# A delta-rule core on one core: its loop of 67 turns written out, and masked copies over tiles that hold the identity in place of two products with it

## Chip, cores and metric

One Trainium2 chip, one of its cores. The metric is the device time of one execution of the whole kernel in microseconds, which is the span of that core; lower is better. Everything is one launch: eight sublayers of a small network over an activation X of 16 x 512 tokens x 128 channels, which stays on the chip between them.

## What is computed

The change touches one part of one sublayer, the chunked delta rule of `L1_attn_b`. There are 16 sequences, 4 heads of 32 channels and chunks of 32 tokens, so 16 chunks for each sequence:

```python
A = jnp.where(strict_lower, jnp.einsum('bhncd,bhnsd->bhncs', k_beta, k), 0.0)
attn_inv = jax.scipy.linalg.solve_triangular(eye + A, jnp.broadcast_to(eye, A.shape), lower=True)
u = attn_inv @ v
w = attn_inv @ k_beta
...
def step(S, inp):
    q_i, k_i, u_i, w_i = inp
    attn_local = jnp.where(incl_lower, q_i @ jnp.swapaxes(k_i, -1, -2), 0.0)
    u_t = u_i - w_i @ S
    o_i = q_i @ S + attn_local @ u_t
    return (S + jnp.swapaxes(k_i, -1, -2) @ u_t, o_i)
```

A is 32 x 32 for each chunk and head, strictly lower triangular; the state S is carried from chunk to chunk.

## The kernel before

The program is a row of stages, each with its own tiles and semaphores and a barrier at its end: attention with a mask (L0), the mixture of experts twice, window attention, attention with rotation, channel mixing twice, and the gated delta sublayer. The last consists of `delta_inputs` (q, k, v), `delta_core`, `long_filters` and `gated_sum`, one after the other. Nothing of another stage runs beside `delta_core`.

**Items and slots.** An item is one chunk of 4 sequences with 4 heads each: 16 blocks of 32 x 32, which fill a slot of 128 partitions (head and row) x 4 sequences x 32 columns. There are 64 items (4 groups of sequences x 16 chunks). `products` (L2424) is one product of slots: 16 matmuls of 32 x 32 in fp32. Each stands in the trace as two weight loads and two matmuls, so a product has 32 and 32 records.

**The inverse.** (I + A)^-1 is built from 2 x 2 blocks upward in levels: `first` is the gram matrix masked to the pairs, `U2` adds the identity. Then, for blocks of 4, 8, 16 and 32 (n = 0 to 3): a product of G1 or G2 (copies of the gram matrix) with U gives the block below the diagonal, DVE masks it out of PSUM into `N[n]` (`masked`, L2532; the masks hold -1 inside and 0 outside), a product of `N[n]` with the transposed T adds to T in PSUM, DVE turns the result by 32 x 32 transposes into `U[n]` (`turn`, L2535), and ACT copies it to `T_[n]`. The levels of 4 and 8 use the banks called early, those of 16 and 32 the ones called late, for the item before. Two products with the identity put the old T into PSUM ahead of the sum: `products(T_early, U2, eye, True)`, whose result ACT also copies to `T2`, and `products(T_late, U[1], eye, True)`; the level's own product then has `fresh` False.

**A turn.** The four engines run a loop of 67 turns (64 items and a lag of 3), in which each product serves another item: the early levels of one, the late levels of the one before, then w and u, then state and output of a third. The order within a turn is written by hand for every engine, and semaphores tie them together. PE has 18 products, DVE 13 operations, ACT 8 copies, POOL 7 operations (chunks of k, q, v out of a ring of tiles, G2, U2). SP is written out already: it fills the ring (3 transfers of 256 KB for 4 items) and stores each item's output in 4 transfers from `out`.

**The loop.** On PE, ACT and POOL it is `Fori(0, TURNS)`, on DVE a `Fori` of 3 turns and then, for each group, a `Fori` of 15 turns and one turn on its own that clears S. Waits are on values that come from the loop's register (`r + 1`, `r + 2`); to keep them positive, semaphores are raised by 1 ahead of the loop, and each group of waits ends with a `sem_inc(waited, 1)`.

Of the kernel before, what the change touches and what calls it, by code (L numbers as in the profile page):

```python
# [6 lines left out]
ACT = mybir.ActivationFunctionType  # L7
# [2284 lines left out]
def delta_core(nc, tag, io, kqv_dram, delta_dram):  # L2292
# [8 lines left out]
    TURNS, LAG = ITEMS + 3, 3  # L2301
    TILE_ITEMS = P // CHUNK
    with Stage(nc, tag) as s:
# [10 lines left out]
        local, w, S, u, out = slot("local"), slot("w"), slot("S"), slot("u"), slot("out")  # L2314
# [7 lines left out]
        kA_ready, qC_ready, kqvB_ready = s.sem("kA_ready"), s.sem("qC_ready_1"), s.sem("kqvB_ready_1")  # L2322
        K_ready, V_ready, G2_ready = s.sem("K_ready_1"), s.sem("V_ready_1"), s.sem("G2_ready_1")
        gram_done, first_ready, G_kept = s.sem("gram_done_1"), s.sem("first_ready_1"), s.sem("G_kept_1")
        U2_ready, T2_done, T2_kept = s.sem("U2_ready_1"), s.sem("T2_done_1"), s.sem("T2_kept_1")
        per_level = lambda name: [s.sem(f"{name}{n}_1_") for n in range(LEVELS)]
        N_done, N_kept = per_level("N_done"), per_level("N_kept")
        T_done, U_kept, T_kept = per_level("T_done"), per_level("U_kept"), per_level("T_kept")
        local_done, local_kept, q_used = s.sem("local_done_1"), s.sem("local_kept_1"), s.sem("q_used_1")
        w_done, w_kept, u_done, u_kept = s.sem("w_done_1"), s.sem("w_kept_1"), s.sem("u_done_1"), s.sem("u_kept_1")  # L2330
        S_done, S_kept, out_done, out_kept = (s.sem("S_done_1"), s.sem("S_kept_1"), s.sem("out_done_1"),
                                              s.sem("out_kept_1"))
        stored = s.sem("stored_4")
        waited = s.sem("waited")
# [9 lines left out]
        def chunk(x, m):  # L2344

            return ring[:, x, :, bass.ds(((m + CHUNKS) % CHUNKS) * CHUNK, CHUNK)]

        @block.sync
        def _(sp):
            sp.dma_start(masks[:, :, :], io["chunk_masks"].rearrange("m p i -> p m i")).then_inc(masks_in, 16)  # L2350
            sp.sem_inc(stored, 64 * (LAG + 1))
# [16 lines left out]
            for m in range(ITEMS):  # L2368
                group, k = m // CHUNKS, m % CHUNKS
                sp.wait_ge(out_kept, m + LAG + 2)  # L2370
                for h in range(DH):
                    rows = slice(CHUNK * h, CHUNK * h + CHUNK)
                    sp.dma_start(delta_dram[group * GROUP:(group + 1) * GROUP, k * CHUNK:(k + 1) * CHUNK, rows]
                                 .rearrange("b i d -> i b d"), out[rows, :, :]).then_inc(stored, 16)
                if m % TILE_ITEMS == 2 and m // TILE_ITEMS + TPS < GROUPS * TPS:
                    load(m // TILE_ITEMS + TPS)
                    if m // TILE_ITEMS + TPS == GROUPS * TPS - 1:
                        sp.sem_inc(ring_in, 48)
            sp.wait_ge(stored, 64 * (LAG + 1 + ITEMS))

        @block.gpsimd
        def _(pool):
# [6 lines left out]
            for sem in (qC_ready, kqvB_ready, G2_ready, U2_ready):  # L2389
                pool.sem_inc(sem, 1)  # L2390
# [5 lines left out]
            with pool.Fori(0, TURNS) as r:  # L2396
                pool.wait_ge(q_used, r + 2)
                pool.sem_inc(waited, 1)
                g.tensor_copy(qC[:, :, :], chunk(Q_ROW, r - 2)).then_inc(qC_ready, 1)
                pool.wait_ge(N_done[3], r + 2)  # L2400
                pool.sem_inc(waited, 1)
                g.tensor_copy(G2[:, :, :], G1[:, :, :]).then_inc(G2_ready, 1)
                pool.wait_ge(first_ready, r + 2)
                pool.sem_inc(waited, 1)
                g.tensor_tensor(U2[:, :, :], first[:, :, :], over(EYE), ALU.add).then_inc(U2_ready, 1)
                pool.wait_ge(gram_done, r + 2)
                pool.sem_inc(waited, 1)
                pool.wait_ge(ring_in, ((r + 1) // TILE_ITEMS) * 48 + 48)
                pool.sem_inc(waited, 1)
                g.tensor_copy(kA[:, :, :], chunk(K_ROW, r + 1)).then_inc(kA_ready, 1)  # L2410
                pool.wait_ge(V_ready, r + 2)
                pool.sem_inc(waited, 1)
# [5 lines left out]
        def _(pe):  # L2418
# [9 lines left out]
            eye = masks[:, EYE, :].unsqueeze(1).to_broadcast([P, GROUP, CHUNK])  # L2428
            for sem in (q_used, S_done, out_done, u_done, local_done, gram_done, T2_done, w_done, *N_done, *T_done):
                pe.sem_inc(sem, 1)  # L2430
# [4 lines left out]
            with pe.Fori(0, TURNS) as r:  # L2435
                now, before = r + 2, r + 1
                pe.wait_ge(U_kept[1], before)
                pe.wait_ge(G2_ready, before)
                pe.wait_ge(local_kept, before)
# [9 lines left out]
                pe.wait_ge(w_kept, before)  # L2449
                pe.wait_ge(S_kept, before)  # L2450
# [4 lines left out]
                pe.sem_inc(waited, 1)  # L2455
                products(T_late, N[2], T_[1], False).then_inc(T_done[2], 1)
                pe.wait_ge(qC_ready, before)
                pe.wait_ge(out_kept, before)
                pe.sem_inc(waited, 1)
# [3 lines left out]
                pe.sem_inc(waited, 1)  # L2463
                products(T_early, N[0], T2, False).then_inc(T_done[0], 1)
# [629 lines left out]
```

## Time and profile before

| | before |
|---|---|
| median of 3 runs | 5331.94 us (5324.82 to 5354.07) |
| the profiled execution | 5354.72 us, span 5352.7 us |
| busy over the span | PE 4147.9 us (77%), PE weight loads 2483.3, DVE 3059.4, ACT 2393.8, POOL 1809.8 |
| delta core | about 4259 to 4702 us of the span |
| PE records | 73,116 matmuls and 73,118 weight loads |
| mean granted clock of PE | 0.854 |

PE is TensorE's matmuls, PEld its weight loads, DVE VectorE, ACT ScalarE, POOL GpSimd, SP the engine that issues most DMAs. In the timelines a row merges neighbouring instructions of one kind: start, duration, and in brackets how long the engine was idle before it, and what ended that; "issue" means that nothing which the profile shows was awaited. The queues q8 and q14 bring instructions, q1 and q0 data.

### The profile page before, as it was taken

Reading aid. Unit: us, or ns where it says so; the run is one execution under the profiler, and the core shown is the slowest. Engines: PE = TensorE matmul, PEld = TensorE weight load, DVE = VectorE, ACT = ScalarE, POOL = GpSimd, SP = SyncE. Lnnn points to the kernel's source line nnn. Section 1 sums busy time; section 2 is a strip of 40 time slices with the busy share of each in tenths; the row PEclk is TensorE's granted clock in tenths of the full one; section 3 lists DMA queues with packets and bytes.
Section 4 is the critical chain, followed back from the end, with each engine's and each line's share of the span. In section 5 each row is a group of like instructions: output and inputs, shape, how many; then the busy total and the mean of one; then the engine's idle time right before and its main releaser. Section 6 shows DMA issues by size and latency. Waiting matters only on the chain. (4 is left out here: it accounts for less than half of the span.)

```text
span 5352.7 us, 179249 instructions
## 1 busy us (share of the span) xinstructions
PE 4147.9 (77%) x73116; PEld 2483.3 (46%) x73118; DVE 3059.4 (57%) x6496; ACT 2393.8 (45%) x5497; POOL 1809.8 (34%) x2620
## 2 busy tenths in 40 slices
PE   4898888448189999997291699999957799996555
PEld 1333333347045555555291233333345699984223
DVE  5555554434366666664344677777576555514887
ACT  1555555125145445552151377777735433313443
POOL 3343433130655555551405332222012233302442
PEclk9888887579599999997595799999877799997777
DMA  2111110211100000001111111111001211162001
GB/s 75 45 46 46 45 47 21 73 52 52 37 2 2 3 2 2 2 2 33 41 53 48 48 45 46 44 48 43 19 2 63 84 39 45 22 193 77 24 24 34
DMA packets 252942, 218.33 MB, mean 41 GB/s; under 512 B 63683, under 2 KB 221316, under 8 KB 252550
## 3 DMA queue, kind: packets, MB, share of 16 engines
q1 hardware_dynamic: 244358, 196.20, 12.1%
q0 software_dynamic: 8192, 16.79, 1.1%
q8 instruction: 259, 4.24, 0.3%
q14 instruction: 133, 1.09, 0.1%
HBM read 139.24 MB, written 73.14 MB: 40 GB/s over the span
## 5 line engine op out<-in xcount | busy, mean ns | idle before, releaser
L687 DVE TENSOR_REDUCE l_M<-l_max_bank 128x2 f32<-128x1024 f32 (+3 forms) x1024 | 1033.6, 1024 | 616.7 <-PE l_max_bank L501 381.7
L647 ACT ACTIVATE l_probs<-l_exp_bank 128x512 f32<-128x512 f32 (+3 forms) x2048 | 953.9, 520 | 632.8 <-PE l_exp_bank L517 622.6
L517 PE MATMUL l_exp_bank<-l_QS,l_KS 49*128 49x512 bf16 (+3 forms) x2048 | 667.4, 369 | 82.0 <-ACT l_probs L647 68.1
L495 PE MATMUL l_max_bank<-l_KS,l_QS 48*128 48x512 bf16 (+3 forms) x2048 | 611.5, 374 | 69.8 <-DMA l_KS<-l_parts_dram 45.2
L479 PE MATMUL l_out_bank<-l_probs,l_V 128*32 128x256 f32 (+2 forms) x6144 | 562.8, 448 | 23.0 <-ACT l_heads_out L603 20.8
L397 POOL TENSOR_SCALAR_AFFINE_SELECT l_probs<-l_probs 128x256 f32<-128x256 f32 x512 | 208.7, 408 | 543.1 <-ACT l_probs L647 540.6
L517 PEld LDWEIGHTS l_exp_bank<-l_QS,l_KS 49*128 49x128 bf16 x2048 | 177.0, 95 | 375.4 <-ACT l_probs L647 350.9
L495 PEld LDWEIGHTS l_max_bank<-l_KS,l_QS 48*128 48x128 bf16 x2048 | 156.4, 97 | 333.3 <-issue 165.7
L1841 DVE TENSOR_REDUCE l_M<-l_max_bank 128x4 f32<-128x512 f32 x256 | 175.5, 686 | 171.7 <-PE l_max_bank L1655 171.7
L871 POOL DMA_INDIRECT l_back<-main_sorted_out,l_index x128 | 122.6, 958 | 412.8 <-issue 412.8
L436 POOL TENSOR_TENSOR l_qk<-l_qk,l_cos 128x512 f32<-128x512 f32 x32 | 40.5, 1266 | 568.7 <-ACT l_rot L621 568.7
L479 PEld LDWEIGHTS l_out_bank<-l_probs,l_V 128*32 128x32 f32 x6144 | 135.0, 111 | 207.8 <-issue 164.2
L1496 POOL TENSOR_TENSOR l_rms<-l_rms,l_minus_half 128x20 f32<-128x20 f32 x64 | 226.2, 3535 | 11.8 <-POOL l_rms L1493 11.6
L501 PE MATMUL l_max_bank<-l_ident,l_mask 64*128 64x64 bf16 x2048 | 228.4, 208 | 0.0
L969 ACT ACTIVATE l_hidden<-l_up_bank,l_own 128x128 f32<-128x128 f32 x584 | 166.9, 368 | 86.7 <-PE l_up_bank L919 86.7
L1721 ACT ACTIVATE l_raw<-l_misc 128x512 f32<-128x512 f32 (+1 forms) x192 | 101.4, 528 | 222.1 <-PE l_misc L1558 220.8
L915 PE MATMUL l_t_bank<-main_identity,l_rows 128*128 128x128 f32 x148 | 49.4, 334 | 185.9 <-DMA l_rows<-main_sorted_in 185.9
L857 POOL DMA_INDIRECT main_sorted_in<-l_hn,l_index x128 | 124.7, 974 | 189.6 <-DVE l_hn L1000 151.2
L1633 PE MATMUL l_out_bank<-l_V,l_probs 64*64 64x65 f32 x2048 | 175.6, 226 | 1.3 <-issue 1.3
L1635 PE MATMUL l_out_bank<-l_V,l_probs 64*64 64x65 f32 x2048 | 175.6, 226 | 0.0
L1641 PE MATMUL l_out_bank<-l_V,l_probs 64*64 64x65 f32 x2048 | 175.6, 226 | 0.0
L501 PEld LDWEIGHTS l_max_bank<-l_ident,l_mask 64*128 64x128 bf16 x2048 | 160.7, 105 | 21.9 <-issue 7.0
(419 smaller groups left out, 10301.3 us busy)
## 6 DMA issues: line engine op xcount, KB each, us to landing
l_parts_dram<-l_parts SPq DMA_DIRECT2D x64, 384.0 KB, 2.6
l_fir_band<-in_dr_short_dram SPq DMA_DIRECT2D x16, 1024.0 KB, 6.6
l_fir_band<-in_dr_long_dram SPq DMA_DIRECT2D x16, 1024.0 KB, 8.9
l_QS<-l_parts_dram SPq DMA_DIRECT2D x128, 96.0 KB
l_KS<-l_parts_dram SPq DMA_DIRECT2D x128, 96.0 KB
l_kqv_dram<-l_in_out SPq DMA_DIRECT2D x16, 768.0 KB, 3.6
l_core_ring<-l_kqv_dram SPq DMA_DIRECT2D x48, 256.0 KB, 3.2
l_rows<-main_sorted_in SPq DMA_DIRECT2D x152, 64.0 KB, 1.8
```

Of the source, the lines that this page charges most:

```text
L397: nc.gpsimd.affine_select(out=diagonal, in_=diagonal, compare_op=ALU.is_ge, fill=0.0, base=0, pattern=[[0, 2], [1, P]], channel_multiplier ...
L479: last = nc.tensor.matmul(out_bank[STRIP * h:STRIP * (h + 1), q0:q1], V[:, par, kb, 4 * j + h, :], probs[:, 2 * kb + h // 2, h % 2, q0:q1] ...
L495: return nc.tensor.matmul(max_bank[:, max_head(b, u, g) % MAX_RING, 0:W[t]], QS[64 * g:64 * g + ROWS, to, i, t * P:(t + 1) * P], KS[64 * g ...
L501: return nc.tensor.matmul(max_bank[:, max_head(b, u, g) % MAX_RING, at:at + 64], mask64[rows, c, :], ident64[rows, :], start=False, stop=T ...
L517: return nc.tensor.matmul(exp_bank[:, exp_head(b, u, n) % EXP_RING, Q0[kb]:T], KS[64 * g:64 * g + ROWS + 1, b.par, i, kb * P:(kb + 1) * P] ...
L647: nc.scalar.activation(probs[:, n, EXP_ORDER[h], Q0[kb]:T], exp_bank[:, e % EXP_RING, Q0[kb]:T], ACT.Exp, scale=float(D) ** -0.5).then_inc ...
L687: nc.vector.reduce_max(M[:, j % 2, col:col + 9:8], max_bank[:, m % MAX_RING:m % MAX_RING + 2, 0:W[t]], AX.X)\
L1496: g.tensor_tensor(rms[:, :], rms[:, :], minus_half[:, :], ALU.pow).then_inc(rms_ready, 1)
L1633: nc.tensor.matmul(o[top], now[top, top], v, start=begin_a or (t == 0 and a == 0), stop=True, skip_group_check=True)
L1635: last = nc.tensor.matmul(o[low], now[top, low], v, start=begin_a, stop=True, skip_group_check=True)
L1641: last = nc.tensor.matmul(o[low], now[low, top], V[low, par, t, j, :], start=begin_a, stop=True, skip_group_check=True)
L1841: v.reduce_max(M[:, t % 2, h:h + REP], max_bank[:, r, :].rearrange("p (a k) -> p a k", a=REP), AX.X).then_inc(max_done, 1)
```

## The change

**Written out.** The `Fori` loops of `delta_core` become Python loops: 67 turns of straight code on PE, ACT, DVE and POOL. Waits are on constants; those for a value of 0 are left out (`wait_positive`), the raised starting values and `waited` go, and addresses in the ring are constants.

**The identity.** The four `N[n]` are filled once with the identity. In each turn `copy_predicated` (`inside`) writes the block out of PSUM over it where the mask is not zero, instead of the multiplication by the mask. N then holds I + N, the product with T needs no sum in PSUM, and the two products with the identity go. Since the copy doesn't change the sign, G1 is copied with a scale of -1. T2, which was ACT's copy of one of these products, becomes a transpose of U2 on DVE at the turn's end, after a wait for POOL's U2.

**The output.** `out` gets two halves, with a semaphore of stores for each.

```diff
@@ sync @@
-                    used = TILE_ITEMS * (g - TPS) + 7
+                    used = TILE_ITEMS * (g - TPS) + 6
...
-                                 .rearrange("b i d -> i b d"), out[rows, :, :]).then_inc(stored, 16)
+                                 .rearrange("b i d -> i b d"), out[rows, (m + LAG) % 2, :, :]).then_inc(stored[(m + LAG) % 2], 16)
@@ gpsimd @@
-            with pool.Fori(0, TURNS) as r:
-                pool.wait_ge(q_used, r + 2)
-                pool.sem_inc(waited, 1)
+            for r in range(TURNS):
+                pool.wait_ge(q_used, r + 1)
                 g.tensor_copy(qC[:, :, :], chunk(Q_ROW, r - 2)).then_inc(qC_ready, 1)
...
@@ tensor @@
-            with pe.Fori(0, TURNS) as r:
-                now, before = r + 2, r + 1
...
+            for r in range(TURNS):
+                before, now = r, r + 1
+                wait_positive(pe, U_kept[1], before)
+                wait_positive(pe, G2_ready, before)
+                wait_positive(pe, local_kept, before)
                 products(late_bank, G2, U[1], True).then_inc(N_done[2], 1)
-                pe.wait_ge(U2_ready, before)
-                pe.wait_ge(T_kept[1], before)
-                pe.sem_inc(waited, 1)
-                products(T_early, U2, eye, True).then_inc(T2_done, 1)
-                pe.wait_ge(G_kept, before)
-                pe.sem_inc(waited, 1)
+                wait_positive(pe, U2_ready, before)
+                wait_positive(pe, G_kept, before)
                 products(early_bank, G1, U2, True).then_inc(N_done[0], 1)
...
                 products(u_bank, w, S, False).then_inc(u_done, 1)
-                products(T_late, U[1], eye, True)
                 pe.wait_ge(N_kept[2], now)
-                pe.sem_inc(waited, 1)
-                products(T_late, N[2], T_[1], False).then_inc(T_done[2], 1)
+                wait_positive(pe, T_kept[1], before)
+                products(T_late, N[2], T_[1], True).then_inc(T_done[2], 1)
...
                 pe.wait_ge(N_kept[0], now)
-                pe.wait_ge(T2_kept, now)
-                pe.sem_inc(waited, 1)
-                products(T_early, N[0], T2, False).then_inc(T_done[0], 1)
+                wait_positive(pe, T2_ready, before)
+                products(T_early, N[0], T2, True).then_inc(T_done[0], 1)
...
@@ scalar @@
-            with act.Fori(0, TURNS) as r:
-                now = r + 2
-                act.wait_ge(T2_done, now)
-                copy(T2, T_early, T2_kept)
+            for r in range(TURNS):
+                now = r + 1
...
-                act.wait_ge(stored, r * 64 + 64)
-                copy(out, out_bank, out_kept)
+                wait_positive(act, stored[r % 2], 64 * ((r - LAG) // 2))
+                copy(out[:, r % 2, :, :], out_bank, out_kept)
...
-                copy(G1, gram_bank, G_kept)
+                copy(G1[:, :, :], gram_bank, G_kept, scale=-1.0)
@@ vector @@
+            def inside(to, x, n, done):
+
+                v.copy_predicated(to[:, :, :], over(n).bitcast(mybir.dt.int32), x).then_inc(done, 1)
...
+            for x in N:
+                last = v.tensor_copy(x[:, :, :], over(EYE))
+            last.then_inc(cleared, 1)
+            dve.wait_ge(cleared, CLEARED)
+            for r in range(TURNS):
...
                 dve.wait_ge(N_done[2], now)
-                masked(N[2], late_bank, 3, N_kept[2])
+                inside(N[2], late_bank, 3, N_kept[2])
...
                 dve.wait_ge(T_done[1], now)
                 turn(U[1], flat(T_early), U_kept[1])
...
+                dve.wait_ge(U2_ready, now)
+                turn(T2, flat(U2[:, :, :]), T2_ready)
```

PE's code of the core before, the head of the loop's body (each row is one product of 16 matmuls; the names are out<-inputs, N0 to N3 all as N, T2 and T4 to T16 as T):

```order
L2435 ISA
L2424 MATMUL l_core_late_bank<-l_core_U,l_core_G 32x32 x16
L2424 MATMUL l_core_T_early_bank<-l_core_masks,l_core_U 32x32 x16
L2424 MATMUL l_core_early_bank<-l_core_U,l_core_G 32x32 x16
L2424 MATMUL l_core_u_bank<-l_core_S,l_core_w 32x32 x16
L2424 MATMUL l_core_T_late_bank<-l_core_masks,l_core_U 32x32 x16
L2454 REGISTER_ALU
L2424 MATMUL l_core_T_late_bank<-l_core_T,l_core_N 32x32 x16
L2424 MATMUL l_core_out_bank<-l_core_S,l_core_qC 32x32 x16
```

And its end, the only one for all turns:

```order
L2424 MATMUL l_core_S_bank<-l_core_U,l_core_K 32x32 x16
L2424 MATMUL l_core_u_bank<-l_core_V,l_core_U 32x32 x16
L2435 REGISTER_ALU
L2435 COMPARE_AND_BRANCH
L31 UNCONDITIONAL_BRANCH
L2222 UNCONDITIONAL_BRANCH
```

Of the change, the end of the first turn and the head of the second:

```order
L2419 MATMUL l_core_S_bank<-l_core_U,l_core_K 32x32 x16
L2419 MATMUL l_core_u_bank<-l_core_V,l_core_U 32x32 x16
L2419 MATMUL l_core_late_bank<-l_core_U,l_core_G 32x32 x16
L2419 MATMUL l_core_early_bank<-l_core_U,l_core_G 32x32 x16
L2419 MATMUL l_core_u_bank<-l_core_S,l_core_w 32x32 x16
L2419 MATMUL l_core_T_late_bank<-l_core_T,l_core_N 32x32 x16
L2419 MATMUL l_core_out_bank<-l_core_S,l_core_qC 32x32 x16
```

The branch and the two products that read `masks` are gone; after the last product of a turn the next turn's code follows, 16 products for each of 67 turns.

DVE's code before, the end of the body in one of its loops:

```order
L2535 STREAM_TRANSPOSE l_core_K<-l_core_kqvB 128x128
L2535 STREAM_TRANSPOSE l_core_U<-l_core_T_late_bank 128x128
L2532 TENSOR_TENSOR l_core_local<-l_core_late_bank,l_core_masks 128x128
L2532 TENSOR_TENSOR l_core_first<-l_core_gram_bank,l_core_masks 128x128
L2535 STREAM_TRANSPOSE l_core_V<-l_core_kqvB 128x128
L2535 STREAM_TRANSPOSE l_core_U<-l_core_T_early_bank 128x128
L2582 REGISTER_ALU
L2582 COMPARE_AND_BRANCH
```

Of the change, the end of a turn and the head of the next:

```order
L2509 STREAM_TRANSPOSE l_core_K<-l_core_kqvB 128x128
L2509 STREAM_TRANSPOSE l_core_U<-l_core_T_late_bank 128x128
L2502 TENSOR_TENSOR l_core_local<-l_core_late_bank,l_core_masks 128x128
L2502 TENSOR_TENSOR l_core_first<-l_core_gram_bank,l_core_masks 128x128
L2509 STREAM_TRANSPOSE l_core_V<-l_core_kqvB 128x128
L2509 STREAM_TRANSPOSE l_core_U<-l_core_T_early_bank 128x128
L2509 STREAM_TRANSPOSE l_core_T<-l_core_U 128x128
L2506 COPY_PREDICATED l_core_N<-l_core_masks,l_core_late_bank 128x128
L2506 COPY_PREDICATED l_core_N<-l_core_masks,l_core_early_bank 128x128
```

The transpose into T2 stands behind the one into U[1], and the next turn begins with the two predicated copies.

## Rows read from the trace of the kernel before

**Rows 1.** The timeline of PE, its last product in the delta core (start us, us, engine, what)
```profile
4701.30 0.45 PE L2424 MATMUL l_core_u_bank<-l_core_V,l_core_U 32*32 32x32 f32 x32
```

**Rows 2.** The timeline of PEld, the loop's first turn
```profile
4259.48 0.52 PEld L2424 LDWEIGHTS l_core_u_bank<-l_core_V,l_core_U 32*32 32x32 f32 x32 [9.66 <-DMA l_core_masks<-in_dr_chunk_masks_dram]
...
4260.41 0.57 PEld L2424 LDWEIGHTS l_core_T_early_bank<-l_core_masks,l_core_U 32*32 32x32 f32 x32
4260.84 0.69 PEld L2424 LDWEIGHTS l_core_early_bank<-l_core_U,l_core_G 32*32 32x32 f32 x32
...
4265.77 0.29 PEld L2424 LDWEIGHTS l_core_out_bank<-l_core_S,l_core_qC 32*32 32x32 f32 x25 [2.81 <-issue]
...
4270.22 0.45 PEld L2424 LDWEIGHTS l_core_out_bank<-l_core_u,l_core_local 32*32 32x32 f32 x26 [2.83 <-issue]
...
4274.66 0.45 PEld L2424 LDWEIGHTS l_core_gram_bank<-l_core_kA 32*32 32x32 f32 x27 [2.65 <-issue]
```

**Rows 3.** The timeline of PEld, one turn in full swing
```profile
4446.49 0.34 PEld L2424 LDWEIGHTS l_core_late_bank<-l_core_U,l_core_G 32*32 32x32 f32 x29 [0.46 <-issue]
...
4450.58 0.37 PEld L2424 LDWEIGHTS l_core_late_bank<-l_core_kqvB 32*32 32x32 f32 x32
4450.87 0.37 PEld L2424 LDWEIGHTS l_core_gram_bank<-l_core_kA 32*32 32x32 f32 x32
4451.17 0.37 PEld L2424 LDWEIGHTS l_core_T_early_bank<-l_core_T,l_core_N 32*32 32x32 f32 x32
...
4452.05 0.37 PEld L2424 LDWEIGHTS l_core_u_bank<-l_core_V,l_core_U 32*32 32x32 f32 x32
4452.88 0.34 PEld L2424 LDWEIGHTS l_core_late_bank<-l_core_U,l_core_G 32*32 32x32 f32 x29 [0.46 <-issue]
```

**Rows 4.** Busy time by stretch
```profile
core 0: us, PE busy (x) PEld busy (x) DVE busy (x) ACT busy (x) POOL busy (x), PEclk, DMA share, GB/s
1700.00:2300.00 600.00, 561.09 (x8311) 338.17 (x8308) 375.37 (x686) 301.84 (x657) 319.90 (x443) 0.97 0.01 2
4270.20:4274.60 4.40, 1.92 (x126) 1.79 (x126) 1.03 (x4) 0.28 (x1) 0.00 (x0) 0.50 0.56 168
4300.00:4700.00 400.00, 375.77 (x36120) 360.88 (x36112) 211.83 (x814) 132.28 (x501) 128.53 (x436) 1.00 0.14 34
4446.45:4452.85 6.40, 6.00 (x576) 5.76 (x576) 3.39 (x13) 2.11 (x8) 2.07 (x8) 1.00 0.09 15
```

**Rows 5.** The DMA queues, stretch 4300 to 4700
```profile
q1 hardware_dynamic: 54729, 13.52, 14.4%
q14 instruction: 3, 0.02, 0.0%
```

**Rows 6.** The page's DMA queues, whole span
```profile
q8 instruction: 259, 4.24, 0.3%
```

**Rows 7.** DMA in 40 slices of the stretch 4262 to 4280
```profile
GB/s 343 335 236 23 0 0 49 140 343 345 346 226 143 182 10 0 0 100 224 345 345 319 341 109 1 0 0 0 0 0 36 0 0 18 0 0 0 0 0 0
```

**Rows 8.** The timeline of PEld, window attention's loop jumping back
```profile
2245.52 0.24 PEld L1605 LDWEIGHTS l_exp_bank<-l_QT,l_KT 64*64 64x64 f32 x8 [3.45 <-issue]
```

**Rows 9.** DMA in 40 slices of 2242.5 to 2246.5, and its instruction queue
```profile
GB/s 0 0 164 0 0 0 0 0 0 0 0 0 0 0 0 82 0 0 0 0 0 0 0 0 0 0 0 0 0 0 0 0 0 164 0 0 0 0 0 0
...
q8 instruction: 2, 0.03, 2.9%
```

**Rows 10.** The timeline of DVE, the turn of rows 3
```profile
4447.04 0.29 DVE L2532 TENSOR_TENSOR l_core_N<-l_core_late_bank,l_core_masks 128x128 f32<-128x128 f32 x1 [1.30 <-PE l_core_late_bank L2424]
...
4448.66 0.32 DVE L2535 STREAM_TRANSPOSE l_core_U<-l_core_T_late_bank 128x128 f32<-128x128 f32 x1 [0.73 <-PE l_core_T_late_bank L2424]
...
4451.16 0.26 DVE L2532 TENSOR_TENSOR l_core_local<-l_core_late_bank,l_core_masks 128x128 f32<-128x128 f32 x1
...
4451.63 0.30 DVE L2535 STREAM_TRANSPOSE l_core_V<-l_core_kqvB 128x128 f32<-128x128 f32 x1
```

**Rows 11.** Who ACT waited for, stretch 4300 to 4700
```profile
ACT l_core_out L2501 <- PE l_core_out_bank L2424: 25.0, 63, 0.4
```

More of the change, by code:

```diff
@@ L2300, in delta_core @@
     FIRST, LOCAL, EYE = 0, LEVELS + 1, LEVELS + 2
-    TURNS, LAG = ITEMS + 3, 3
+    LAG = 3
+    TURNS = ITEMS + LAG
     TILE_ITEMS = P // CHUNK
@@ L2313, in delta_core @@
         N = [slot(f"N{n}") for n in range(LEVELS)]
-        local, w, S, u, out = slot("local"), slot("w"), slot("S"), slot("u"), slot("out")
+        local, w, S, u = slot("local"), slot("w"), slot("S"), slot("u")
+        out = s.sb("out", [P, 2, GROUP, CHUNK])
         bank = lambda name: s.ps(name, [P, T])[:, 0:GROUP * CHUNK].rearrange("p (b n) -> p b n", n=CHUNK)
@@ L2344, in chunk, with tiles_in @@
         def chunk(x, m):
-            return ring[:, x, :, bass.ds(((m + CHUNKS) % CHUNKS) * CHUNK, CHUNK)]
+            at = (m % CHUNKS) * CHUNK
+            return ring[:, x, :, at:at + CHUNK]
+        def tiles_in(m):
+            return 48 * (min(m, ITEMS - 1) // TILE_ITEMS + 1)
         @block.sync
@@ L2476, in _ @@
                 pe.wait_ge(T_kept[2], now)
-                pe.sem_inc(waited, 1)
-                products(T_late, N[3], T_[2], False).then_inc(T_done[3], 1)
-                pe.wait_ge(kqvB_ready, before)
-                pe.sem_inc(waited, 1)
+                products(T_late, N[3], T_[2], True).then_inc(T_done[3], 1)
+                wait_positive(pe, kqvB_ready, before)
                 products(late_bank, kqvB[:, K_ROW, :, :], kqvB[:, Q_ROW, :, :], True).then_inc(local_done, 1)
-                pe.wait_ge(kA_ready, before)
-                pe.sem_inc(waited, 1)
+                pe.wait_ge(kA_ready, now)
                 products(gram_bank, kA, kA, True).then_inc(gram_done, 1)
@@ L2486, in _ @@
                 pe.wait_ge(T_kept[0], now)
-                pe.sem_inc(waited, 1)
-                products(T_early, N[1], T_[0], False).then_inc(T_done[1], 1)
+                products(T_early, N[1], T_[0], True).then_inc(T_done[1], 1)
                 pe.wait_ge(U_kept[3], now)
@@ L2532, in masked @@
                 v.tensor_tensor(to[:, :, :], x, over(n), ALU.mult).then_inc(done, 1)
+            def inside(to, x, n, done):
+                v.copy_predicated(to[:, :, :], over(n).bitcast(mybir.dt.int32), x).then_inc(done, 1)
             def turn(to, x, done):
                 v.transpose(flat(to[:, :, :]), x).then_inc(done, 1)
-            def turns(r, last_of_group=False):
-                now = r + 2
+            for x in (U2, *U, T2, *T_):
+                last = v.memset(x[:, :, :], 0.0)
+            last.then_inc(cleared, 1)
+            for x in (local, w, S, u):
+                last = v.memset(x[:, :, :], 0.0)
+            last.then_inc(cleared, 1)
+            dve.wait_ge(masks_in, 16)
+            for x in N:
+                last = v.tensor_copy(x[:, :, :], over(EYE))
+            last.then_inc(cleared, 1)
+            dve.wait_ge(cleared, CLEARED)
+            for r in range(TURNS):
+                before, now = r, r + 1
+                item = r - LAG
                 dve.wait_ge(N_done[2], now)
-                masked(N[2], late_bank, 3, N_kept[2])
+                inside(N[2], late_bank, 3, N_kept[2])
                 dve.wait_ge(N_done[0], now)
-                masked(N[0], early_bank, 1, N_kept[0])
+                inside(N[0], early_bank, 1, N_kept[0])
                 dve.wait_ge(T_done[2], now)
@@ L2547, in turns @@
                 dve.wait_ge(N_done[3], now)
-                masked(N[3], late_bank, 4, N_kept[3])
+                inside(N[3], late_bank, 4, N_kept[3])
                 dve.wait_ge(S_done, now)
-                if last_of_group:
+                if item >= 0 and item % CHUNKS == CHUNKS - 1:
                     v.memset(S[:, :, :], 0.0).then_inc(S_kept, 1)
@@ L2554, in turns @@
                 dve.wait_ge(N_done[1], now)
-                masked(N[1], early_bank, 2, N_kept[1])
-                dve.wait_ge(kqvB_ready, r + 1)
+                inside(N[1], early_bank, 2, N_kept[1])
+                wait_positive(dve, kqvB_ready, before)
                 turn(K, flat(kqvB[:, K_ROW, :, :]), K_ready)
@@ L2562, in turns @@
                 dve.wait_ge(gram_done, now)
-                dve.wait_ge(U2_ready, r + 1)
+                wait_positive(dve, U2_ready, before)
                 masked(first, gram_bank, FIRST, first_ready)
@@ L2567, in turns @@
                 turn(U[1], flat(T_early), U_kept[1])
-            for x in (U2, *U):
-                last = v.memset(x[:, :, :], 0.0)
-            last.then_inc(cleared, 1)
-            for x in (T2, *T_, *N):
-                last = v.memset(x[:, :, :], 0.0)
-            last.then_inc(cleared, 1)
-            for x in (local, w, S, u):
-                last = v.memset(x[:, :, :], 0.0)
-            last.then_inc(cleared, 1)
-            for sem in (K_ready, V_ready, first_ready, local_kept, S_kept, *N_kept, *U_kept):
-                dve.sem_inc(sem, 1)
-            dve.wait_ge(masks_in, 16)
-            dve.wait_ge(cleared, CLEARED)
-            with dve.Fori(0, LAG) as r:
-                turns(r)
-            for n in range(GROUPS):
-                with dve.Fori(0, CHUNKS - 1) as i:
-                    turns(i + (LAG + n * CHUNKS))
-                turns(LAG + n * CHUNKS + CHUNKS - 1, n < GROUPS - 1)
+                dve.wait_ge(U2_ready, now)
+                turn(T2, flat(U2[:, :, :]), T2_ready)
 SOURCES = 4
```

81 lines of the change are left out of this document (27 added, 54 removed).

## The prediction

> **What bounds the kernel now.** I read four views in this order: the page, to place the stage in the whole; the busy time by stretch, for how densely each stage issues; the timeline of PEld and DVE for one turn in full swing; and the timeline of PEld for the first turn of the loop with the DMA view beside it. The profiled execution took 5354.7 us, 22.8 above the median of 5331.9 and next to the slowest of the three; the sum is made against it, and the 22.8 are taken off at the end.
>
> The delta core runs from its first product at 4259.48 to the last one at 4701.30 plus 0.45 [rows 1, 2]: 442 us for 67 turns. Nothing else runs beside it, so what a turn gains or loses is gained or lost by the kernel, 67 times. A turn takes 6.39 us, from 4446.49 to 4452.88 [rows 3]. PE is busy for 6.00 of 6.40 us, DVE for 3.39, ACT for 2.11, POOL for 2.07 [rows 4]: the stage hangs on how fast TensorE gets through its 18 products. Products that wait for nothing stand 0.29 to 0.30 us apart (4450.58, 4450.87, 4451.17); the last product of a turn and the first of the next stand 0.83 apart (4452.05 to 4452.88), 0.46 of it idle for "issue" [rows 3]. That is the loop's price.
>
> The reader should next see how many instructions this is. The turn has 576 weight loads and 576 matmuls [rows 4], 64 for each product. In the stretch 4300 to 4700 PE ran 72,232 of them, and the instruction queue q8 moved nothing: it isn't in the list, only three small q14 pieces are [rows 5]. The loop's body stays where the engine reads it. All the rest of the program needed 259 pieces of q8, 4.24 MB, so 16.4 KB each [rows 6].
>
> **What straight-line code costs here.** The first turn of this loop had to be brought in, and the trace shows it as PE met it. PEld stops in the middle of a product, though nothing is awaited: 2.81 us before 4265.77, 2.83 before 4270.22, 2.65 before 4274.66, each "issue" [rows 2]. Between two restarts lie 126 weight loads and 126 matmuls [rows 4]; with the waits that stand among them that is one piece of 16.4 KB, some 256 instructions of 64 bytes. So at this density PE gets 256 instructions per 4.44 us, where a turn in full swing uses 1152 in 6.39, which is 256 per 1.42. The pieces did not run ahead: the period is neither execution alone nor many pieces at once. I read it as one piece asked for when the one before it is entered, and arriving 4.45 us later.
>
> How much of the 4.45 is load? The DMA engines carried ring tiles then, at 340 GB/s in bursts [rows 7]. An unloaded case is in window attention: its loop jumps back and PE stands still for 3.45 us [rows 8] with almost nothing else on the DMA engines, and the next piece of q8 follows the first after 31 slices of 0.1 us, 3.1 us [rows 9]. That gives 3.1 to 3.45 us unloaded, 4.45 behind ring tiles. Elsewhere in straight code this doesn't show, because PE asks for less: window attention executes 16,619 in 600 us, 256 per 9.2 us [rows 4], more than the latency.
>
> **The change, part by part.**
> - Written out. A turn has 16 products left, 1024 PE instructions, and some 16 waits that stand as instructions of their own: 1040, or 4.06 pieces. 67 turns are 272 pieces, where the loop's body was some five. Each piece takes the longer of the latency and its own execution. Execution is 4 products of 0.30, 1.2 us, or 1.7 at the lower clock of the first turns (0.43 from 4260.41 to 4260.84, where the granted clock stood near 0.50, which is 1.2 GHz [rows 2, 4]), so the latency decides. I take 3.45 us, the row that shows a whole standstill without load: 272 x 3.45 = 938. The bounds are 3.1 (843) and 4.45 (1210). For load I add 0.9 us for each of the 16 groups of ring tiles that a piece can meet, 15 us. The stage is then 953 us instead of 442: **+511**.
> - The loop's jump (0.46 of idle time and the register work around it) and two products of about 0.3 go. Were PE bound by its own work, that would be worth about 1 us a turn (first rival). Here PE waits some 2.2 us for each piece whatever it executes, so only the number of instructions counts: the two products are 128 of them, half a piece, 1.7 us a turn that a written-out core with 18 products would cost on top. The sum has that already.
> - Four masked copies. Before: a multiply from PSUM at 0.29 [rows 10]. The page of before has no predicated copy; its nearest rows are 0.26 (local) and 0.32 (a transpose), and if it read its target in a second pass it could be twice 0.29. I take 0.29, and keep 0 to +0.29 for each. Cover: DVE has 3.4 busy of 14.2 us per turn. Without the cover, four times 0.1 would be at most 0.4 us a turn, 27 us.
> - The transpose for T2 moves from a copy on ACT to the end of DVE's turn, behind U[1] and behind POOL's U2. It adds 0.3 busy us to DVE; queued behind it is N[2] of the next turn, which waits for PE anyway. Zero.
> - G1 with a scale of -1, stores into two halves of `out`: ACT's waits name PE and DVE only, no store; for the output it is PE [rows 11]. Zero.
> - DVE, ACT, POOL and SP also read straight code, but with some 30 instructions a turn or fewer; a piece lasts them several turns. Zero.
>
> The Trainium skill, page "Runtime: NRT & Kernel Launch", section "Instruction fetch mechanics", says that an engine fetches its next 16 KiB block while it executes the current one, that this is mostly hidden, and that kernels had better be unrolled, since a taken branch breaks the sequential prefetch. By that rule the sum would be the first rival's. The trace agrees on the block's size and on the price of a branch; the three stalls of 2.65 to 2.83 us in straight code speak against "hidden" at this density.
>
> Sum: 5354.7 + 511 = 5865.7 on the profiled execution's footing, less 22.8: **5843 us**, +9.6%.
>
> **The rivals.**
> 1. Pieces run ahead in a long straight stretch, and fetching stays hidden. Then PE's own work decides: 16 x 0.30 = 4.8, plus 0.36 because the last product waits for V, which DVE turns after first (gram to V's end took 4450.87 to 4451.93, and 0.12 to the product [rows 3, 10]), plus about 0.2 at two other hand-overs: 5.4 us a turn. The gain is 67 x 0.99 = 66: 5266 us, faster. For it: window attention at half the density never stalls, and the first turn may be special, since it follows a jump and shares its DMA engines. Against: window attention never comes near this density and so proves nothing about it, and three stalls of nearly one length are no accident of load. It decides from the point where a piece arrives in under 1.35 us. Chance 0.10.
> 2. Two pieces are in flight at once, so one comes every 1.75 us: 272 x 1.75 = 476, +34: 5366. For it: at the start more than one piece could be run before the first stall. Against: the 3.1 us of [rows 9] and the 4.45 of [rows 2] are single file. Chance 0.04.
> 3. Every piece costs the loaded 4.45, because the gap of 4.45 isn't load but execution plus a fetch begun too late: 1210, +768: 6100. For it: the three periods agree closely although the bursts of load don't. Against: PE runs slow code without a stall at each piece, so something is fetched ahead. Chance 0.06.
> That the change doesn't do what it says is excluded for its form: the order shows turn after turn with no branch.
>
> **How the numbers follow.** 0.5% (27 us) is about what a measurement can tell. The forecast has 0.80, the rivals 0.10, 0.04 and 0.06. Faster is the first rival alone, 0.10; slower is the rest, 0.89, with 0.01 for a time in between. The range leaves out rivals 1 and 2 (0.14). Its lower end is the 3.1 us of [rows 9], 5332 + 401 = 5733, less some 80 for a latency down to 2.8, the bare stall of [rows 2]; its upper end takes in rival 3: 5650 to 6100.
>
> **What would show it.** q8 with about 525 pieces instead of 259; PEld idle for "issue" some 2 us about every four products, in the middle of products, and 500 to 650 us of it in the stage; turns of about 14 us that vary with where a piece ends; DVE idle for most of a turn, waiting for PE. A turn of 5.4 us with idle time put down to V would make the prediction wrong, as would a q8 count that doesn't rise.

## The result, and the profile after

| | before | changed |
|---|---|---|
| median | 5328.38 us (5319.39 to 5354.07, 4 runs) | 5926.73 us (5920.01 to 5948.14, 4 runs) |
| ratio | | 1.112 [1.107, 1.117] |
| the profiled execution | 5354.72 us | 5924.38 us |
| delta core, first to last product | 4259.48 to 4701.75: 442.3 us | 4247.20 to 5274.03: 1026.8 us |
| PE busy over the span | 4147.9 us (77%) | 4253.9 us (72%) |
| mean granted clock of PE | 0.854 | 0.787 |
| pieces in q8 | 259 | 525 |

The kernel is 598 us slower by the medians, 569.7 by the two profiled executions. The core alone is 584.5 longer. The stages before it ended 12.3 us earlier, those after it took 2.3 less, and neither was touched by the change. So all of the loss is in the core.

The page of the changed kernel, its busy time and its two instruction queues, which answer to [rows 6]:

```profile
PE 4253.9 (72%) x68830; PEld 2573.3 (43%) x68830; DVE 3097.0 (52%) x6563; ACT 2372.9 (40%) x5430; POOL 1803.3 (30%) x2620
...
q8 instruction: 525, 8.60, 0.6%
q14 instruction: 150, 1.22, 0.1%
```

PE shows 4286 matmuls fewer (the two products with the identity are 2 x 32 x 67 = 4288) and is busy for longer. q8 moved 266 more pieces, all of 16.4 KB.

Busy time by stretch of the changed kernel, answering to [rows 4] (columns as there: PE, PEld, DVE, ACT, POOL, granted clock, DMA share, GB/s):

```profile
4247.20:5285.00 1037.80, 531.61 (x34354) 493.73 (x34354) 262.76 (x938) 124.06 (x471) 133.41 (x472) 0.50 0.09 23
4600.00:4900.00 300.00, 151.84 (x9936) 141.41 (x9927) 76.18 (x272) 35.93 (x138) 38.94 (x138) 0.50 0.09 22
4605.70:4609.70 4.00, 1.92 (x127) 1.79 (x127) 0.93 (x3) 0.55 (x2) 0.59 (x2) 0.50 0.01 4
```

Before, PE was busy for 376 of 400 us and ran 72,232 instructions; now it is busy for half the time, and 300 us see 19,863 instructions, 66 for each us instead of 181. DVE is busy for a quarter of the stage, ACT and POOL for an eighth. No engine is full, and the DMA engines are at 9%. The granted clock is 0.50, 1.2 GHz, where it was 1.00. The last row holds one piece: 127 weight loads and 127 matmuls in 4.0 us.

The waits of PEld in the changed core (what waited, for what, us in total, times, longest):

```profile
PEld l_core_late_bank L2419 <- issue: 94.4, 48, 2.4
PEld l_core_T_early_bank L2419 <- issue: 77.6, 39, 2.2
PEld l_core_early_bank L2419 <- issue: 75.5, 38, 2.9
PEld l_core_S_bank L2419 <- issue: 68.5, 34, 2.5
PEld l_core_u_bank L2419 <- issue: 67.9, 34, 3.2
PEld l_core_T_late_bank L2419 <- issue: 67.2, 34, 2.7
PEld l_core_out_bank L2419 <- issue: 58.4, 29, 2.8
PEld l_core_gram_bank L2419 <- issue: 28.0, 14, 2.5
```

Together that is 537.5 us in 270 stalls, 1.99 us each. They fall on the products about as often as each stands in a turn (late three times, gram once, the others twice; 270/16 is 17 for each): the stall belongs to a place in the code, not to what is computed. No wait for DVE, ACT or POOL is in the view; besides these lines it has only the wait for the masks ahead of the first product.

The timeline of PEld in the changed core answers to [rows 2] and [rows 3]:

```profile
4602.11 0.34 PEld L2419 LDWEIGHTS l_core_u_bank<-l_core_V,l_core_U 32*32 32x32 f32 x17 [1.70 <-issue]
...
4603.63 0.27 PEld L2419 LDWEIGHTS l_core_T_late_bank<-l_core_T,l_core_N 32*32 32x32 f32 x9
4605.79 0.34 PEld L2419 LDWEIGHTS l_core_T_late_bank<-l_core_T,l_core_N 32*32 32x32 f32 x18 [1.90 <-issue]
...
4607.32 0.26 PEld L2419 LDWEIGHTS l_core_S_bank<-l_core_u,l_core_K 32*32 32x32 f32 x9
4609.79 0.34 PEld L2419 LDWEIGHTS l_core_S_bank<-l_core_u,l_core_K 32*32 32x32 f32 x19 [2.21 <-issue]
```

PE runs four products in 1.8 us, stops in the middle of one for 1.9 to 2.2, and goes on. From restart to restart it takes 3.68 and 4.00 us. The DMA engines in the same 8 us of the changed kernel, in 40 slices of 0.2 us, and the instruction queue there:

```profile
GB/s 0 0 0 0 0 0 82 0 0 0 0 0 0 0 0 0 0 0 0 0 0 0 0 0 0 0 82 0 0 0 0 0 0 0 0 0 0 0 0 0
...
q8 instruction: 2, 0.03, 1.7%
```

These are the parts of a piece's latency, to the 0.2 us of a slice. It begins to move 1.1 to 1.4 us after PE restarted in the piece before it (4602.11 to slice 6, which begins at 4603.2; then 4605.79 to slice 26, at 4607.2; a packet is counted in the slice in which it begins). Its packet occupies one DMA engine for 1.09 us (1.7% of 16 x 8 us, in two). Some 1.5 us later PE is running again. Between one piece and the next, the DMA engines are idle for most of the time.

DVE in the changed core, grouped by form, stretch 4300 to 5200 (times | busy us, mean ns | idle before):

```profile
L2506 DVE COPY_PREDICATED l_core_N<-l_core_masks,l_core_late_bank 128x128 f32<-128x128 int32 x117 | 35.1, 300 | 170.7 <-PE l_core_late_bank L2419 166.1
...
L2509 DVE STREAM_TRANSPOSE l_core_T<-l_core_U 128x128 f32<-128x128 f32 x59 | 17.7, 300 | 4.9
L2502 DVE TENSOR_TENSOR l_core_local<-l_core_late_bank,l_core_masks 128x128 f32<-128x128 f32 x59 | 17.2, 291 | 34.1 <-PE l_core_late_bank L2419 29.2
```

The masked copy takes 0.30 us where the multiplication took 0.29 [rows 10], and waits for PE 1.5 us on average (170.7/117). The transpose into T2 takes 0.30 and hardly ever waits.

### The profile page after: what moved, and what is told of

Read it like the earlier page. It is cut to its first block and busy times, and to the rows that moved or that the text cites. A ratio compares the mean times of both kernels' runs of the same rounds, so it can differ in the third digit from the quotient of the medians.

```text
span 5922.7 us, 168351 instructions
## 1 busy us (share of the span) xinstructions
PE 4253.9 (72%) x68830; PEld 2573.3 (43%) x68830; DVE 3097.0 (52%) x6563; ACT 2372.9 (40%) x5430; POOL 1803.3 (30%) x2620
```

## The experiments

Nine kernels ran beside the kernel before, on three chips. Where one run was made, its time is a single one; the effects it shows are then hundreds of us.

### e1: the arithmetic of the change, with the loops kept

```diff
 with pe.Fori(0, TURNS) as r:
...
-    products(T_early, U2, eye, True).then_inc(T2_done, 1)
...
-    products(T_late, U[1], eye, True)
...
-    products(T_late, N[2], T_[1], False).then_inc(T_done[2], 1)
+    products(T_late, N[2], T_[1], True).then_inc(T_done[2], 1)
...
-    masked(N[2], late_bank, 3, N_kept[2])
+    dve.sem_inc(dve_waited, 1)
+    inside(N[2], late_bank, 3, N_kept[2])
...
+    dve.wait_ge(U2_ready, now)
+    turn(T2, flat(U2[:, :, :]), T2_ready)
```

> The loops stay as in the kernel before; only the identity part of the change is made (predicated copies over tiles that hold the identity, 16 products, T2 as a transpose on DVE). DVE's four copies each get a semaphore increment of their own behind the wait. Theory of code (PE waits for instruction pieces of 256, about 3.8 us each): with the loop the code stays, q8 stands near 260 pieces, a turn falls from 6.39 to about 5.9 us and the time to about 5295 us. Theory of the chain (the predicated copies and the T2 transpose lengthen the hand-overs between DVE and PE): most of the 598 us stay, about 5900 us with turns of 14 to 15 us.

Measured: 5301.84 us (5290.93 to 5322.77, 8 runs), ratio 0.9944 [0.9923, 0.9964]; the core took 403.2 us, 39.1 less than before's. The timeline of PEld over one turn of e1:

```profile
4443.87 0.34 PEld L2424 LDWEIGHTS l_core_late_bank<-l_core_U,l_core_G 32*32 32x32 f32 x29 [0.48 <-issue]
...
4448.43 0.37 PEld L2424 LDWEIGHTS l_core_S_bank<-l_core_U,l_core_K 32*32 32x32 f32 x32
4448.90 0.37 PEld L2424 LDWEIGHTS l_core_u_bank<-l_core_V,l_core_U 32*32 32x32 f32 x32
4449.72 0.34 PEld L2424 LDWEIGHTS l_core_late_bank<-l_core_U,l_core_G 32*32 32x32 f32 x29 [0.44 <-issue]
```

A turn takes 5.85 us instead of 6.39: the two products gone, 0.54 us. The wait for V before the last product shows as 0.47 between 4448.43 and 4448.90 where free products stand 0.29 apart, and the jump costs its 0.44 still. So this half of the change is worth a gain, and without the jump a turn would take 5.4 us, what the first rival reckoned. The loss is due to the other half: from e1's core of 403.2 us to the changed one of 1026.8 it costs 624 us, of which 39 are hidden by the gain of this half.

### e2: before, with PE's loop alone written out

```diff
-with pe.Fori(0, TURNS) as r:
+for r in range(TURNS):
```

> The kernel before, its arithmetic unchanged with 18 products, with PE's code alone written out (DVE, ACT and POOL keep their loops). Theory of code: 67 turns of 1170 instructions are 306 pieces at 3.8 us, 1165 us for the core instead of 442, so about 6050 us, and q8 near 565 pieces. Theory of the chain: as the kernel before, 5330 us or a little less. Theory of the other engines (the written-out code of DVE, ACT or POOL comes late): 5330 us too.

Measured: 6087.37 us (1 run); the core took 1204.3 us. On its page, and the three largest waits of PEld over its core:

```profile
q8 instruction: 560, 9.18, 0.6%
```

```profile
PEld l_core_late_bank L2424 <- issue: 115.1, 55, 2.6
PEld l_core_T_late_bank L2424 <- issue: 109.8, 52, 3.3
PEld l_core_T_early_bank L2424 <- issue: 102.3, 49, 3.1
```

One line of one engine makes the loss and more: 301 pieces more than before, the same stalls, 1204.3 / 306 = 3.9 us for each piece (301 and the loop's five). The products, their order and the other engines' code are those of before. With 18 products the written-out core is 177 us longer than with 16: 35 pieces more at 3.8 us are 133, and the other 44 are that a piece took 3.94 us on average and not 3.80, for which no reason was looked for.

### e3: before, with all loops but PE's written out

```diff
-with pool.Fori(0, TURNS) as r:
+for r in range(TURNS):
...
-with act.Fori(0, TURNS) as r:
+for r in range(TURNS):
...
-with dve.Fori(0, LAG) as r:
-    turns(r)
+for r in range(LAG):
+    turns(r)
...
-    with dve.Fori(0, CHUNKS - 1) as i:
+    for i in range(CHUNKS - 1):
```

> The kernel before with the code of DVE, ACT and POOL written out, PE's loop kept. Theory of code on PE: within 20 us of the kernel before. Theory of the other engines: 5800 us or more.

Measured: 5321.53 us (5304.16 to 5343.43, 10 runs), ratio 0.9976 [0.9961, 0.9991]; the core took 442.6 us and q8 259 pieces, both as before. Straight code on these three engines costs nothing. The 0.24% by which the kernel is faster doesn't come from the core; stages before the core, of the same code, took between 4226 and 4259 us in the profiled executions, and what moved them wasn't settled.

### e4: the changed kernel with half the matmuls of each product

```diff
+groups = [GROUP]
...
-for b in range(GROUP):
+for b in range(groups[0]):
...
     products(u_bank, U[3], V, True)
+    groups[0] = GROUP // 2
```

> The changed kernel, but from the second turn on each product issues only 8 of its 16 matmuls (the blocks of two of the four sequences are left out and keep old values). PE's code halves: about 2.05 pieces a turn. If the time goes by pieces (3.8 us each whatever they hold), the core falls from 1037 to about 67 x 2.05 x 3.8 = 520 us and the time to about 5410 us. If it went by hand-overs between the engines, which stay as many, it would stay within 100 us of 5927.

Measured: 5437.16 us (1 run); the core took 548.4 us, with 393 pieces in q8: 134 more than before, so some 139 in the core, 3.9 us each. The stretch 4300 to 4700 of e4:

```profile
4300.00:4700.00 400.00, 228.35 (x12703) 199.55 (x12704) 173.67 (x694) 89.93 (x348) 99.07 (x349) 0.50 0.15 34
```

Half the instructions, 0.53 of the time, at 64 instructions for each us again. The turns come nearly twice as fast, and DVE with them (0.43 of the stretch instead of 0.25), which excludes any limit that goes by turns, semaphores or DVE's work. What is left goes by the number of PE's instructions or by their execution, which was halved as well; the next run takes these two apart.

### e5: the changed kernel with matmuls four times as wide

```diff
-last = nc.tensor.matmul(o[rows, b, :], a[rows, b, :], x[rows, b, :],
+last = nc.tensor.matmul(whole[id(o)][rows, :, b, :], a[rows, b, :],
+                        x[rows, b, :].unsqueeze(1).to_broadcast([CHUNK, WIDE, CHUNK]),
```

> The changed kernel with every matmul of the core four times as wide (32 x 128 instead of 32 x 32; three copies beside the result that nothing reads). As many instructions, longer to execute. In the changed kernel's trace a piece has 1.7 us of execution and a stall of 2.1, 3.8 in all. If the next piece is asked for when a piece is entered, the stall shrinks by what execution grows and the period stays at 3.8 as long as execution stays under it (time within 60 us of 5927); if it is asked for when a piece is used up, the period grows with execution: with execution at 3.0 us it would be 5.1, and the time near 6280.

Measured: 5945.72 us (1 run); the core took 1043.7 us, 524 pieces. Busy time by stretch, then the timeline of PEld, in e5:

```profile
4600.00:4900.00 300.00, 279.56 (x9636) 260.52 (x9631) 74.41 (x264) 34.72 (x133) 37.61 (x133) 1.00 0.08 19
```

```profile
4601.53 0.37 PEld L2427 LDWEIGHTS l_core_T_late_bank<-l_core_T,l_core_N 32*32 32x32 f32 x15 [1.48 <-issue]
...
4602.73 0.92 PEld L2427 LDWEIGHTS l_core_T_early_bank<-l_core_T,l_core_N 32*32 32x32 f32 x32
4603.60 0.92 PEld L2427 LDWEIGHTS l_core_late_bank<-l_core_U,l_core_G 32*32 32x32 f32 x32
...
4612.23 0.46 PEld L2427 LDWEIGHTS l_core_u_bank<-l_core_V,l_core_U 32*32 32x32 f32 x17 [0.22 <-issue]
...
4616.31 0.47 PEld L2427 LDWEIGHTS l_core_T_late_bank<-l_core_T,l_core_N 32*32 32x32 f32 x18 [0.66 <-issue]
```

PE now is busy for 93% of the time instead of 51%, at a granted clock of 1.00 instead of 0.50, and the stage takes 1.6% more. Four products at 0.87 us (4602.73 to 4603.60) are 3.5 us of execution for each piece, and PEld's idle time for "issue" in the core shrank from 537.5 to 106.5 us in sum. The work went into the time in which PE had waited. Two things follow. The next piece is not asked for only when the present one is done: had the 2 us of each stall been a fetch that begins behind the execution, a period would have been 5.5 us, and the core some 1,490. And the low clock is not what makes the stage slow.

e5 leaves open whether a piece is asked for at the entry of the one before it, or as soon as the one before it has arrived; with PE always short of code the two are the same. The kernel before tells them apart in window attention, where a piece is executed in some 9 us. Behind the jump of [rows 8] two packets begin 3.1 us apart, at 2242.7 and 2245.8 [rows 9]. The DMA engines of the kernel before in 40 slices of 1 us from there, 2246 to 2286:

```profile
GB/s 8 0 0 0 0 0 0 8 0 16 0 0 0 0 0 0 0 16 0 0 0 0 0 0 0 0 16 0 0 0 0 0 0 0 16 0 0 0 0 0
...
q8 instruction: 4, 0.07, 0.7%
```

The four pieces (16 each; the 8s are q14's) begin in slices 9, 17, 26 and 34, so 8 to 9 us apart, although the queue could have brought one each 3.1 us and PE holds more than six (e7 below). PE asks for one piece as it enters the one before it, and for no more.

### e6: e1 with two turns in the body of PE's loop

```diff
-with pe.Fori(0, TURNS) as r:
+with pe.Fori(0, TURNS // 2) as i:
+    turn_of(i * 2)
+    turn_of(i * 2 + 1)
+turn_of(TURNS - 1)
```

> The loop with the predicated copies, with PE's body made two turns long (33 rounds and one turn behind it): some 2090 instructions, 8.2 pieces, where the body of one turn has 4.1. If what PE holds is enough for it, a turn saves half of the loop's jump, 0.25 us, 17 us in all against the body of one turn. If it holds only about 8 pieces, the body is brought in anew each round: 4.1 pieces a turn at 3.8 us, as slow as the written-out core, near 5900 us.

Measured: 6113.31 us (6102.18 to 6117.01, 4 runs), ratio 1.146 [1.142, 1.149]; the core took 1212.5 us, q8 moved 587 pieces. The timeline of PEld over one round of e6, some of its restarts:

```profile
4609.42 0.55 PEld L2424 LDWEIGHTS l_core_late_bank<-l_core_U,l_core_G 32*32 32x32 f32 x32 [5.07 <-issue]
4611.97 0.41 PEld L2424 LDWEIGHTS l_core_u_bank<-l_core_S,l_core_w 32*32 32x32 f32 x24 [1.47 <-issue]
4615.66 0.44 PEld L2424 LDWEIGHTS l_core_late_bank<-l_core_U,l_core_G 32*32 32x32 f32 x25 [1.90 <-issue]
...
4638.19 0.19 PEld L2424 LDWEIGHTS l_core_T_early_bank<-l_core_T,l_core_N 32*32 32x32 f32 x6 [2.02 <-issue]
4644.88 0.55 PEld L2424 LDWEIGHTS l_core_late_bank<-l_core_U,l_core_G 32*32 32x32 f32 x32 [5.51 <-issue]
```

A loop with a body of some 2090 instructions for PE is fetched anew each round, and is slower than the core written out. Its 8.2 pieces take ten fetches (587 less 258 is 329, in 33 rounds), and the jump itself stands for 5.1 and 5.5 us in the two rows above, 5.9 at the longest of the run. The expectation had counted 8.2 fetches and no more for the jump, and so came out some 210 us short.

### e8, e7 and e9: where the body stops fitting

e8 is e1 with DVE, ACT and POOL written out as in e3, and without the semaphore increments that e1 has ahead of DVE's masked copies. e7 and e9 are e8 with nine and with fourteen more products in PE's body (the diff of e7; e9 has 14 for 9):

```diff
+for _ in range(9):
+    products(gram_bank, kA, kA, True)
 products(gram_bank, kA, kA, True).then_inc(gram_done, 1)
```

> The loop with the predicated copies on PE, with the code of DVE, ACT and POOL written out. From the two parts measured apart (ratio 0.9944 for the predicated copies in loops, 0.9976 for the other engines' code written out) about 0.992 of the kernel before, 5290 us, if they add. If the written-out code of DVE had hidden only its own loop's jump, which the PE's jump now hides as well, it would stay at 0.994.

> The same kernel with nine more products of kA with itself in PE's body, whose result the tenth replaces: some 1620 instructions, 6.3 pieces. If the body still stays where PE reads it, a turn is 5.8 + 9 x 0.30 = 8.5 us, the time about 5290 + 180 = 5470 us, and q8 near 260 pieces. If it doesn't, a turn costs 7 or more pieces of 3.8 us and a jump, about 29 us: 6850 us or more, and q8 over 700 pieces.

> The same with fourteen more products: some 1940 instructions, 7.6 pieces, against 8.2 in the body of two turns that was brought in anew each round. If it stays: a turn of 5.8 + 14 x 0.30 = 10 us, about 5570 us and q8 near 260. If it doesn't: 9 pieces a turn of 3.8 us, some 7250 us, and q8 over 800.

| | instructions in PE's body | pieces in q8 | core | core / 67 | time |
|---|---|---|---|---|---|
| e8 | some 1040 | 258 | 398.1 us | 5.94 us | 5286.54 us (5278.93 to 5297.93, 4 runs), ratio 0.990 [0.988, 0.992] |
| e7 | some 1620 | 260 | 565.7 us | 8.4 us | 5474.73 us (1 run) |
| e9 | some 1940 | 856 | 2142.6 us | 32 us | 7029.18 us (1 run) |

The restarts of PEld in e9, the end of one turn and the head of the next:

```profile
4608.69 1.79 PEld L2424 LDWEIGHTS l_core_gram_bank<-l_core_kA 32*32 32x32 f32 x128 [1.74 <-issue]
4612.44 1.80 PEld L2424 LDWEIGHTS l_core_gram_bank<-l_core_kA 32*32 32x32 f32 x128 [1.95 <-issue]
...
4620.20 0.45 PEld L2424 LDWEIGHTS l_core_gram_bank<-l_core_kA 32*32 32x32 f32 x27 [1.96 <-issue]
4626.16 0.55 PEld L2424 LDWEIGHTS l_core_late_bank<-l_core_U,l_core_G 32*32 32x32 f32 x32 [4.10 <-issue]
```

Busy time by stretch in e8 and in e9, 4300 to 4600:

```profile
4300.00:4600.00 300.00, 280.07 (x26681) 267.37 (x26668) 192.80 (x729) 95.34 (x364) 103.80 (x365) 1.00 0.17 41
```

```profile
4300.00:4600.00 300.00, 136.06 (x8866) 126.34 (x8857) 37.49 (x131) 17.48 (x68) 19.23 (x68) 0.50 0.06 14
```

A body of 1620 instructions stays, one of 1940 doesn't, and nothing lies between: for 20% more instructions a turn takes almost four times as long. The old loop, with 1152 instructions for its products, was well inside. e8 is the fastest kernel of the study. It beats the kernel before by 1.0% and the changed one by 11%: it has all of the change but PE's straight code and the two halves of `out`. 44 us of its gain are the core's. Its core is 5.1 us shorter than e1's (398.1 against 403.2), where the same straight code gave nothing in e3; whether DVE's missing increments or the straight code gave these 5 us wasn't tried.

## Why the prediction was right, and where it was off

The forecast was 5843 us with 5650 to 6100 around it; the measured median is 5926.73. Mechanism and sign were right: PE is bound by the fetching of its code. The runs show this from four sides: e2 makes the loss by PE's loop alone, e3 shows that the other loops don't matter, e4 scales it with the number of instructions, e5 shows that the work within a piece is free up to the piece's latency.

**The step that was mis-sized: "I take 3.45 us".** The core took 1026.8 us for 270 pieces, 3.80 each, where the forecast had 3.45 for 272 and 15 for load. 3.80 lies between the bounds of 3.1 and 4.45. The term is 0.35 x 272 = 95 us too small; of that 15 come back, since 3.80 has the load in it already, and some 7 for the two pieces fewer: 953 forecast, 1026.8 measured, +74.

The 3.45 was one jump of window attention [rows 8], and the trace of the kernel before has five of them, in the same stage and with as little on the DMA engines. The first one:

```profile
1742.37 0.33 PEld L1605 LDWEIGHTS l_exp_bank<-l_QT,l_KT 64*64 64x64 f32 x8 [3.92 <-issue]
```

The others end at 1867.88 (3.81 us), 1993.82 (3.91), 2119.74 (3.73) and 2245.52 (3.45): 3.76 on average, and the row taken was the shortest. 272 x 3.76 is 1023 us, within 4 us of the core that was measured, and with the 15 for load 1038, within 12. So the way of reading the latency from a jump's standstill held; one row out of five, and the lowest, did not.

**The load.** The sum had 0.9 us for each group of ring tiles. The timeline of PEld in the changed kernel, five restarts around the arrival of one group:

```profile
4270.35 0.34 PEld L2419 LDWEIGHTS l_core_late_bank<-l_core_U,l_core_G 32*32 32x32 f32 x17 [2.01 <-issue]
4273.71 0.34 PEld L2419 LDWEIGHTS l_core_T_late_bank<-l_core_T,l_core_N 32*32 32x32 f32 x17 [1.56 <-issue]
4277.22 0.34 PEld L2419 LDWEIGHTS l_core_S_bank<-l_core_U,l_core_K 32*32 32x32 f32 x18 [1.72 <-issue]
4281.96 0.34 PEld L2419 LDWEIGHTS l_core_u_bank<-l_core_S,l_core_w 32*32 32x32 f32 x19 [2.96 <-issue]
4285.56 0.35 PEld L2419 LDWEIGHTS l_core_late_bank<-l_core_U,l_core_G 32*32 32x32 f32 x19 [1.81 <-issue]
```

And the DMA engines of the changed kernel in 40 slices of 4276 to 4284:

```profile
GB/s 0 0 0 0 0 0 0 0 0 0 0 31 72 253 320 356 338 343 425 320 246 184 164 236 251 243 110 56 20 20 23 20 23 0 0 82 0 0 0 0
```

The period with the tiles in it, 4277.22 to 4281.96, is 4.74 us; its neighbours are 3.36, 3.51 and 3.60. So the load goes with some 1.2 us more in this one, near the 0.9 of the forecast, and would account for the 4.45 in the kernel before [rows 2]. With 16 groups it hardly matters for the sum. No run took the load away, so its price is read from these neighbours alone.

**The number of pieces.** 272 in the core against five, so about 525 in all: 525 on the page, and 270 stalls.

**What was costed at nothing or little.** The masked copies were taken at 0.29 with 0 to +0.29 as bounds: 0.30, so the target isn't paid for a second time. The transpose into T2: 0.30, with 4.9 us of waiting over 59 of them. The straight code of DVE, ACT and POOL: zero, by e3 (442.6 against 442.3).

**The stages around.** The forecast took them as unchanged. They took 14.6 us less in the profiled execution; so +584.5 in the core is some +570 in the executions. The medians differ by 598 because before's profiled execution stands 26.3 above its median, and the changed kernel's 2.4 below.

**The rivals.** 1, fetching stays hidden: refuted by q8, the 270 stalls and e2. Its arithmetic was right where it can be tested: e1's turn of 5.85 less the jump's 0.44 is the 5.4 it reckoned, and e1 shows that two products fewer are worth 39 us of the core where nothing is fetched. The Trainium skill, page "Runtime: NRT & Kernel Launch", section "Instruction fetch mechanics", has this rival's rule, that the next 16 KiB block is fetched while the current one executes and the fetch mostly hidden. The first half agrees with e5, where 3.5 us of execution fitted into a period of 3.8. The second half holds as long as a block's execution outlasts the fetch, 3.8 us, which 256 instructions of small products at 0.3 us for 64 don't; where the measurement and "mostly hidden" differ, the measurement decides. Its advice to prefer unrolled code is wrong for this loop by 762 us, the core of e2 against that of before. 2, two pieces in flight: refuted, a period would have been 1.8 us, and between two packets of q8 the queue stands still for 2.9 us. 3, every piece 4.45 because the fetch begins too late: refuted by the mean of 3.80, and by e5, whose execution of 3.5 us a piece would have lengthened the core by nearly half and did so by 1.6%.

**The clock.** The forecast reckoned execution at both levels, 1.2 us and 1.7, found both under the latency, and left the clock out of the sum. It fell to 0.50 for the whole stage, and e5, at 1.00 for as long a time, shows that it costs nothing here: it makes execution longer (four products in 1.8 us instead of 1.2) inside a latency of 3.8. In e4, whose pieces are the same length, it is the same.

**What stays open.** What sets the 1.1 to 1.4 us before a piece's packet and the 1.5 behind it wasn't tried. Nor was where between 1620 and 1940 instructions the limit for a resident body lies, and whether it goes by the body alone or also by how it is placed.

## What to carry to other kernels

Count the instructions of a stage, not its operations, before writing a loop out: an fp32 product of 16 blocks of 32 x 32 is 64 instructions on PE, and straight code on PE got 256 of them per 3.8 us here, some 67 for each us; a stage that issues more had better stay a loop. Keep that loop's body within some 1600 instructions; two turns in one body, some 2090, cost more than no loop at all. When a latency is read from a trace, read all its occurrences: of five jumps the forecast took one, the shortest, and that was nearly all of its error. Judge the parts of a change apart: the arithmetic here was worth 0.6% and, with the light engines written out and PE's loop kept, 1.0%, while one line on PE cost 14%.

## What the runs showed of the hardware that was not expected

- A loop whose body just doesn't fit is worse than straight code: its jump stands for 4.1 us in e9 and 5.1 to 5.5 in e6, where the five jumps in window attention took 3.45 to 3.92 and the jump of a resident body 0.44 to 0.48. e6's ten fetches for 8.2 pieces say that some of what is fetched around the jump isn't used.
- The limit is abrupt: 8.4 us a turn with 1620 instructions, 32 us with 1940.
- Four times the columns through TensorE cost 1.6% of the stage (1043.7 against 1026.8 us) and brought its granted clock from 0.50 to 1.00: work within a fetched piece costs almost nothing as long as its execution, 3.5 us in e5, stays under the latency of 3.8.
- PE's busy share is blind to this. It reads 51% in the changed core, 93% in e5 for nearly the same time; the stalls show only as idle time for "issue", and in q8's count.
